# A four-layer graph and expert network: TensorE's waits for emptied banks placed at the products that read them, and layer 1's graph stage in another order

## The reference

```python
x = x + _L0_gnn_ref(_layernorm(x), ...)      # mean of neighbours, two 256x256 products
x = x + _L0_ffn_ref(_layernorm(x)[None], ...)[0]  # attention, then 8 experts, top 2
x = x + _L1_gnn_ref(_layernorm(x), src, dst, edge_type_2, ...)
x = x + _L1_ffn_ref(...)[0]                  # 8 experts, top 2
x = x + _L2_gnn_ref(...)                     # graph attention, 8 heads
x = x + _L2_ffn_ref(...)[0]                  # 8 experts, top 2, all of them computed
x = x + _L3_gnn_ref(...)                     # three levels down, with two SAGE products and a
                                             # pooling to half the nodes on each, two levels up
x = x + _L3_ffn_ref(...)[0]                  # one hidden layer of 1024, one of 8 outputs
```

```python
def edge_nn(x, W, b):
    h = jax.nn.relu(x @ W.T + b)
    return jax.nn.relu(h @ W.T + b)
for r in range(2):
    msgs = jnp.where((rel == r)[:, None], edge_nn(S, W_rel[r], b_rel[r]), msgs)
agg = jax.ops.segment_sum(msgs, dst, num_segments=n_nodes)
gates = agg @ W_ih.T + b_ih + b_hh
i, f, g, o = jnp.split(gates, 4, axis=-1)
c = jax.nn.sigmoid(i) * jnp.tanh(g)
hn = jax.nn.sigmoid(o) * jnp.tanh(c)
x = jax.nn.relu(hn @ W1.T + b1)
x = jax.nn.relu(x @ W2.T + b2)
return x @ W3.T + b3
```

## Time and profile before

| | |
|---|---|
| runs, us | 991.3, 986.12, 988.94; median 988.94 |
| profiled execution: span, us | 982.4 (its time beyond the span is not given; the median of the runs is 6.5 us above the span) |
| TensorE busy | 894.5 us, 91% of the span |
| VectorE, ScalarE, GpSimd busy | 441.9, 281.5 and 181.5 us |
| TensorE's mean granted clock | 0.966 of full speed |
| DMA | 120.34 MB, a mean of 123 GB/s |

### The profile page before, as it was taken

How to read it: one execution, slowest core, us unless ns; L and a number is a source line. 1 busy time by engine, 2 the same in 40 slices (tenths; PEclk the granted TensorE clock), 3 DMA queues, 4 the chain that set the end, 5 groups by cost and what they waited for, 6 DMA issues and landing times.

```text
span 982.4 us, 15310 instructions
## 1 busy us (share of the span) xinstructions
PE 894.5 (91%) x5583; PEld 723.0 (74%) x5583; DVE 441.9 (45%) x1402; ACT 281.5 (29%) x625; POOL 181.5 (18%) x177
## 2 busy tenths in 40 slices
PE   7999998999999899799986778999999998889897
PEld 7997656889999767688875667777887554565765
DVE  6688655522222420542278985422435142340623
ACT  5110362122222114133247862323111111114210
POOL 2100000122221200034427752000100100000231
PEclk9999999999999999999998989999999999899899
DMA  8203001288894603159351000353100100320595
GB/s 315 118 1 90 1 1 37 96 303 312 324 327 178 230 0 129 53 168 306 118 162 77 1 1 1 119 176 123 65 0 3 31 1 1 128 94 35 191 358 225
DMA packets 28001, 120.34 MB, mean 123 GB/s; under 512 B 5401, under 2 KB 10032, under 8 KB 20132
## 3 DMA queue, kind: packets, MB, share of 16 engines
q1 hardware_dynamic: 22362, 104.39, 30.1%
q0 software_dynamic: 5280, 14.95, 4.5%
q10 hardware_dynamic: 295, 0.14, 0.1%
HBM read 106.11 MB, written 13.36 MB: 122 GB/s over the span
## 4 chain that ended last, share of the span: by engine, by line
PE 76%; DVE 13%; issue 4%; ACT 3%; DMA 3%; POOL 1%; DVEq 0%; SPq 0%; POOLq 0%; ACTq 0%
PE PS L783 8%; PE PS L454 6%; PE PS L600 5%; PE PS L431 5%; PE PS L798 5%; PE PS L848 4%; PE PS L465 4%; PE PS L834 4%; PE PS L525 4%; PE PS L916 3%; PE PS L905 3%; PE PS L870 2%; PE PS L1226 2%; DVE ring L1933 2%; PE PS L1006 2%
## 5 line engine op out<-in xcount | busy, mean ns | idle before, releaser
L431 PE MATMUL PS<-const 128*128 128x128 f32 x682 | 90.3, 292 | 5.8 <-DVE X L1316 2.1
L431 PEld LDWEIGHTS PS<-const 128*128 128x128 f32 x682 | 86.0, 206 | 10.1 <-DVE X L1316 2.9
L783 PE MATMUL PS<-HT,ring 128*128 128x128 f32 x680 | 79.1, 275 | 3.3 <-DVE HT L1470 1.7
L783 PEld LDWEIGHTS PS<-HT,ring 128*128 128x128 f32 x680 | 78.4, 192 | 4.6 <-issue 3.9
L2593 POOL TENSOR_TENSOR col<-col,power 125x4 f32<-125x4 f32 (+2 forms) x13 | 11.9, 918 | 319.1 <-DVE col L1309 232.0
L2653 POOL DMA_INDIRECT slot_rows<-ST,route x41 | 41.5, 1011 | 149.5 <-ACT ST L2367 95.9
L2691 POOL TENSOR_TENSOR arena<-arena,ring 125x625 f32<-125x625 f32 x40 | 55.7, 1416 | 33.1 <-ACT arena L2455 28.9
L1856 DVE TENSOR_TENSOR HT<-HT,PS 128x256 f32<-128x256 f32 (+1 forms) x51 | 19.1, 377 | 89.7 <-ACT HT L2356 71.6
L600 PE MATMUL PS<-HT 125*125 125x250 bf16 x470 | 51.7, 271 | 0.0
L600 PEld LDWEIGHTS PS<-HT 125*125 125x125 bf16 x470 | 50.5, 137 | 0.1
L798 PE MATMUL PS<-ring,HT 128*128 128x256 f32 x204 | 46.8, 380 | 0.0
(11 more groups left out here) (466 smaller groups left out, 1696.4 us busy)
## 6 DMA issues: line engine op xcount, KB each, us to landing
ring<-in_experts SPq DMA_DIRECT2D x17, 1386.0 KB
ring<-in_experts SPq DMA_DIRECT2D x17, 768.0 KB, 6.1
ring<-in_experts SPq DMA_DIRECT2D x11, 1026.0 KB
arena<-in_experts SPq DMA_DIRECT2D x10, 1024.0 KB
ring<-in_experts SPq DMA_DIRECT2D x7, 1024.0 KB, 6.3
arena<-in_experts SPq DMA_DIRECT2D x6, 1026.0 KB
arena<-in_gnn SPq DMA_DIRECT2D x5, 1024.0 KB, 5.9
ring<-in_experts SPq DMA_DIRECT2D x8, 513.0 KB, 3.7
```

What stands on the lines that cost most here:

```text
L431: pe.matmul(PS[:, bank, 0:128], ident, ident, start=True, stop=True)
L783: mm = pe.matmul(PS[:, bank, at:at + SLOTS], both[:, j, k, m * 128:(m + 1) * 128], xs[0][i % 2][:, k, :], start=(k == 0), stop=(k == KD - 1))
```

## The change

It has three parts.

1. `emptied()` goes behind `transposes` and in `sage_sums`, and so do the waits for all banks in `bias2`, `logits_turned`, `select_targets` and `chosen_targets`. In their place `turned_tile(t)` waits ahead of tile 0 for the first part of the turned rows and ahead of tile 4 for the second; the others wait by tile or half, ahead of the first product that reads it.
2. Layer 1's graph stage makes the hidden rows of both types first (type 1's into ST2, which lies in MB), and then the messages of both. The sums of the messages wait tile by tile, the gates by half. ScalarE takes tanh of the first cell block between the gates of blocks 4 and 5, VectorE multiplies the last block by halves, and the products with w1, w2 and w3 wait by half.
3. The filler ahead of w1 goes from 10 products to 6.

Nothing is computed otherwise. `sage_sums(adj, rows_, fresh)` with `fresh` true stands where `select_targets` comes between: then the products of the first output tile wait for each tile of the new adjacency.

```diff
             def transposes(src, rows_=N, wait=True, busy=0):
-                ts = tiles(rows_)
+                ts, parts = tiles(rows_), []
...
                     mm[1].then_inc(act_full, 1)
+                    parts.append((n["v"], n["a"]))
+                turned_parts[:] = [parts[0], parts[-1]]
+
+            def turned_tile(t):
+
+                if t in (0, 4):
+                    v, a = turned_parts[t // 4]
+                    pe.wait_ge(dve_free, v)
+                    pe.wait_ge(act_free, a)
...
-            def sage_sums(adj, rows_):
+            def sage_sums(adj, rows_, fresh):
                 ts = tiles(rows_)
-                emptied()
                 for t, c0, c in ts:
                     bank = dve_bank()
                     for s, s0, sc in ts:
+                        if t == 0 and (fresh or s == 0):
+                            pe.wait_ge(act_free, n["a"] - (len(ts) - 1 - s if fresh else 0))
...
             def logits_turned(src_t, w, kk):
+                pe.wait_ge(act_free, n["a"] - 1)
                 for c0, c in HALVES:
                     bank = act_bank()
+                    if c0:
+                        pe.wait_ge(act_free, n["a"] - 2)
...
                 bank = dve_bank()
-                pe.wait_ge(act_free, n["a"])
                 for t, c0, c in tiles(N):
+                    if t in (0, HALF_TILES[1][0]):
+                        pe.wait_ge(act_free, n["a"] - (t == 0))
...
             def bias2(which):
...
-                pe.wait_ge(act_free, n["a"])
...
                 for t in range(NT):
                     bank = dve_bank()
+                    if t in (0, 4):
+                        pe.wait_ge(act_free, n["a"] - (t == 0))
...
             def layer1_gnn():
                 transposes(XN, busy=62)
-                emptied()
...
+                hidden_at = []
                 for r in range(2):
-                    feature_major(w_rel[:, r], KD, KD, XT)
-                    pe.wait_ge(act_free, n["a"])
+                    feature_major(w_rel[:, r], KD, KD, XT, first=(lambda half: turned_tile(4 * half)) if r == 0 else None)
+                    hidden_at.append(n["a"])
+                for r in range(2):
+                    pe.wait_ge(act_free, hidden_at[r])
                     for t, c0, c in tiles(N):
                         bank = dve_bank()
-                        root_tile(bank, ST, w_rel[:, r], c0, c).then_inc(dve_full, 1)
-                pe.wait_ge(msg_ready, 2 * NT)
+                        root_tile(bank, (ST, ST2)[r], w_rel[:, r], c0, c).then_inc(dve_full, 1)
...
                             for s in range(NT):
+                                if m == 0 and half == 0:
+                                    pe.wait_ge(msg_ready, r * NT + s + 1)
...
-                pe.wait_ge(act_free, n["a"])
-                pe.sem_inc(gnn_weights_used, 1)
-                feature_major(wv(w1, W1, "w_ih", KD), KD, 6, ST)
+                summed_at = n["a"]
+                def summed(half):
+                    pe.wait_ge(act_free, summed_at - 1 + half)
+                    if half:
+                        pe.sem_inc(gnn_weights_used, 1)
+                feature_major(wv(w1, W1, "w_ih", KD), KD, 6, ST, first=summed)
                 pe.wait_ge(dve_free, n["v"])
-                stay_busy(4 + n["v"] % 4, 10)
-                pe.wait_ge(cell_ready, 2)
-                feature_major(wv(w1, W1, "w1", KD), KD, 1, XT)
-                pe.wait_ge(act_free, n["a"])
-                feature_major(wv(w1, W1, "w2", 1), 1, 1, ST[:, 0:1, :])
-                pe.wait_ge(act_free, n["a"])
+                stay_busy(4 + n["v"] % 4, 6)
+                feature_major(wv(w1, W1, "w1", KD), KD, 1, XT, first=lambda half: pe.wait_ge(cell_ready, 2 + half))
+                first_at = n["a"]
+                feature_major(wv(w1, W1, "w2", 1), 1, 1, ST[:, 0:1, :], first=lambda half: pe.wait_ge(act_free, first_at - 1 + half))
                 for t, c0, c in tiles(N):
+                    if t in (0, HALF_TILES[1][0]):
+                        pe.wait_ge(act_free, n["a"] - (t == 0))
...
             def chosen_targets(rows_, kept):
+                ts, copied = tiles(rows_), n["a"]
                 for kt, k0, kc in tiles(kept):
                     bank = act_bank()
-                    for t, c0, c in tiles(rows_):
+                    for t, c0, c in ts:
+                        if kt == 0:
+                            pe.wait_ge(act_free, copied - (len(ts) - 1 - t))
...
                     def combine(wl, wr_, other):
                         for t, c0, c in ts:
+                            turned_tile(t)
...
+                                    if t == 0 and j:
+                                        pe.wait_ge(act_free, n["a"] - (KD - 1 - k))
...
                 for k in range(KD):
-                    dve.wait_ge(gates_ready, 8 + 2 * k + 2)
+                    dve.wait_ge(gates_ready, 4 + 2 * k + 2)
                     dve.tensor_tensor(ST2[:, k, :], lstm[:, k, :], lstm[:, 2 + k, :], ALU.mult).then_inc(cell_in, 1)
                 for k in range(KD):
                     dve.wait_ge(cell_tanh, k + 1)
-                    dve.tensor_tensor(XT[:, k, :], lstm[:, 4 + k, :], ST2[:, k, :], ALU.mult).then_inc(cell_ready, 1)
+                    for half, (c0, c) in enumerate(HALVES if k else ((0, N),)):
+                        dve.wait_ge(gates_ready, 8 + 2 * k + (half + 1 if k else 2))
+                        dve.tensor_tensor(XT[:, k, c0:c0 + c], lstm[:, 4 + k, c0:c0 + c], ST2[:, k, c0:c0 + c],
+                                          ALU.mult).then_inc(cell_ready, 1)
...
-                for k in range(KD):
-                    act.wait_ge(cell_in, k + 1)
-                    act.activation(ST2[:, k, :], ST2[:, k, :], ACT.Tanh).then_inc(cell_tanh, 1)
+                    if m >= 4:
+                        act.wait_ge(cell_in, m - 3)
+                        act.activation(ST2[:, m - 4, :], ST2[:, m - 4, :], ACT.Tanh).then_inc(cell_tanh, 1)
```

32 lines of the change are left out of this document (14 added, 18 removed).

## The result

| | before | changed |
|---|---|---|
| runs of the first comparison: median, us | 990.12 (986.12 to 991.72, 4 runs) | 975.12 (974.79 to 978.9, 4 runs) |
| ratio of the runs | | 0.9861 (95%: 0.9823 to 0.9899) |
| all runs of this study: mean, us | 989.3 (983.1 to 997.0, 53 runs) | 976.9 (973.5 to 982.0, 14 runs) |
| their mean granted clock | 0.9582 (on record for 49 of them) | 0.9561 |
| profiled execution: span, us; clock | 982.4; 0.966 | 972.7 (its own time 974.79); 0.958 |

What follows compares the result with a forecast made beforehand. TensorE, busy for 91% of the span and carrying 76% of the chain, was taken as the bound. Gains of 4.7 + 1.8 + 6.5 = 13.0 us off the median of 988.94 gave 976 us, range 971 to 981.5.

Steps and rivals of the forecast that it cites:

- The forecast's own case: Whole kernel: 10 to 16 us less than before, chance 0.66.
- Layer 1's graph stage: From hidden rows to w3: new order and waits by tile or half remove TensorE's waits, 4.7 us less.
- The tail's terms: Layer 1, last gate to w3: gates to w1 shortened by 1.1 us, w2's wait by 0.56, w3's by 0.5.
- the size of a stand: Where TensorE waits: removing a wait gains the idle time shown, such as 0.56 or 0.84 us.
- Turned rows: Nine places behind transposes: the first part's copy is ready 0.2 us earlier at each, 1.8 us in all.
- The rest: SAGE sums, `chosen_targets`, `combine`, layer 3's outputs and their turning, `bias2`: unneeded or late waits go, 6.5 us less.
- The turning of the outputs: Layer 3, line 499: three of five small products start at once, the fourth waits as before; 0.4 us less.
- Added waits: TensorE's 25 more waiting instructions cost nothing; at most 52 ns each, 1.3 us, kept for the range.
- Swallowed: Behind logits, `bias2` and the last turning, TensorE only reaches other waits sooner; 8 us less, 981 us, chance 0.15.
- The clock returns more: Whole kernel: fewer short stands spare three half-clock stretches, 4.5 us more gained, 971 us, chance 0.12.
- Slower by the clock in layer 1's stage: Layer 1's graph stage: TensorE falls to half clock with less filler, up to 1009 us, chance 0.02.
- The mean clock at 0.966: Changed kernel's profile: the mean granted clock stays at 0.966, as a sign that the forecast is right.

Runs made afterwards that it cites:

- this part alone: Kernel before with only layer 1's graph stage in its new order and waits and the filler of 6; ratio 0.995, 5.7 us less at equal clock.
- the version with both waits: Changed kernel with the wait for all banks put back behind the turned rows, besides the change's own; ratio 0.9877, 12.9 us less than before at equal clock.
- the second profile: Changed kernel itself, unaltered, with more runs and profiled again; ratio to before 0.9891, median 977.21 us.
- the filled stands: Changed kernel with rows turned in parts of three and two tiles, plus three constant products per stand; 971.2 us, as without them.

## Why the prediction was right, point by point

The predicted time was 976.0; the changed kernel's median was 975.1 in the first comparison and 977.2 in the second. The forecast's own case, 10 to 16 us less, is what came. But two errors of opposite sign met in it: the places of the change gave 14.5 us by starts where 13.0 were forecast, and the changed kernel's runs had a mean clock lower by 0.002, worth 1.6 us, which the forecast didn't have. That they cancel to 12.4 is luck, and so is how near 976.0 lies; that the time fell inside the range is not.

- **Layer 1's graph stage**, 4.7 forecast, 5.7 measured, in the changed kernel and with this part alone. Each step went as described: no stand ahead of either set of messages, none ahead of sums and gates, w1 2.37 us behind the last gate's start, w1 to w3 in 3.75 (388.17 to 391.92) where 3.8 was said. The tail's terms were right to 0.2 (3.43 to 2.37 us from the last gate's start to w1, 1.06 for 1.1; w2 0.73 for 0.56 and w3 0.38 for 0.5). What failed is the size of a stand: I took the idle time shown, 0.56 or 0.84, and each cost 0.72 or 1.0, with up to 0.10 more at the second instruction behind it.
- **Turned rows**, 1.8 forecast, 1.5 measured, twice. Seven of the nine places gave 0.14 to 0.25, two (layer 2's products and the last layer) 0.03. The four SAGE stages whose rows have one part, put at nothing, took 0.13 longer together.
- **The rest**, 6.5 forecast, 7.3 measured. `sage_sums`, `chosen_targets` and `combine` were undersized for the same reason. The turning of the outputs was right, 0.41 for 0.4, and in the way described: 0.71 gained ahead of its first product, of which the fourth gives back 0.3. `bias2` was oversized: three times 0.07 and not 0.16. In the changed kernel its product starts as the pair of copies ends (678.76 against 678.04 + 0.73 in layer 2), and why the end of the first copy isn't enough is not shown.
- **Added waits** were set at nothing, with 1.3 us kept for the range. In rows of products nothing is right. The bound rested on 229 ns against 216 for a message product, and that was a misreading: 4.58 us for 20 instructions holds the last one's modelled tail and the late second instruction behind the stand. By starts they are 4.20/19 = 221 ns apart, one step of 318 ns and 18 of 216. The prediction said that no row shows an extra semaphore instruction. That is so of the views alone; the packed trace of before holds 318. Behind a stand they do cost something, as the version with both waits shows.
- **The size of a stand** is then the one step at fault. In layer 1's stage, `sage_sums`, `chosen_targets` and `combine` it makes 2.1 us together; turned rows and `bias2` gave 0.6 less than forecast, and the table's sums differ by the remaining 1.5.
- **Swallowed** (0.15, at 981): at most 0.7 us is, at the gathers of layer 1's experts and of the last layer's, and nothing in the second profile. The logits and what follows them passed their gain on.
- **The clock returns more** (0.12, at 971): it did not. Taking out these stands left the mean clock where it was or 0.002 lower. The thought behind it was half right, though: filling further stands did raise the clock, by 0.006. The Trainium skill, TensorE: Matmul & The Clock Gate, section A second HAM failure mode: psum-queue depth-cycling, speaks of short idles between groups of products; the filled stands agree with it, the change itself shows no such gain.
- **Slower by the clock in layer 1's stage** (0.02): the stage ran free of low stretches in the changed kernel's profile, with six products of filler as with ten. In five of the other versions, two of them with the stage as before, one low stretch of 3.4 us fell on its first hidden rows.
- **The mean clock at 0.966** in the changed profile was named as a sign of being right. That sign was badly chosen. It was 0.958, and 0.966 was an unusually high value for before, whose 49 runs with a clock on record lie from 0.951 to 0.964. Likewise the 6.5 us that I set between the profiled span and the median of before was no fixed part around the span (the changed kernel's is 974.79 - 972.7 = 2.1) but mostly the clock.

## What to carry to other kernels

Read the cost of a stand by starts: from the start of the last product ahead to the start of the first behind, less the pace of the row. The idle time shown leaves out the overlap of neighbouring products, here 160 ns each time, which for waits of half a microsecond is over a fifth of the gain. A wait that is satisfied costs nothing in a row of products that runs without a break, so place it at the product that reads, once and not twice (behind a stand two more semaphore instructions took 0.15 us), as finely as the copies are made, and then cut the copies so that the first one is small. And where single executions differ by 1% through the clock, compare runs at their mean clock before looking for a cause in one pair of profiles.

## What the runs showed of the hardware

- A float32 matmul instruction of 257 columns stands with 381 ns and is followed after 216 to 222 ns in a row; behind a stand the start to start time is the idle time, plus 0.38. The second instruction behind a stand starts after 290 ns where it is 221 without (257 columns), and after 318 for 216 (256 columns).
- 81 further instructions with a satisfied wait, 23 of them with a second, lengthened the rows of 50 instructions by nothing (11.03 us and 11.03 us), although TensorE's queue then held 35 semaphore instructions of mostly 51 ns in these loops instead of 7. Where TensorE had stood still, two more of them lengthened the step by 0.15 to 0.18 us at each of four places.
- The mean granted clock of before's runs went from 0.951 to 0.964 with nothing changed, and the time with it: 994.4 us on average below 0.955, 984.6 at 0.963 and above. The span spent at the lower level was 65 to 106 us in the profiles of this study.
- Three products of a constant in each of 15 places, most of them with stands of under a microsecond, raised it from 0.959 to 0.965, and the time stayed where it was.
